# Replicated q and k copied in two halves by heads, maxima over six feed-forward blocks

## The chip, the core and the metric

One core of a Trainium2 chip runs the whole program. The metric is the device time in microseconds; lower is better. Engines are named TensorE (PE, with its weight loads PEld), VectorE (DVE), ScalarE (ACT), GpSimd (POOL) and SyncE (SP). Each has a queue of its own, executes it in order, and waits on semaphores.

## What is computed

Eight sequences x of 512 tokens with 256 channels each. First a cross attention with 16 heads on 64 context tokens, added to x. Then, of the normalised result, a dense path and a sparse path:

```python
q, k, v = x @ wq, x @ wk, x @ wv                     # 16 heads of 16
attn = softmax(where(causal, q k^T / 4, min))
h = x + rmsnorm((attn @ v) @ wo)
dense = h + rmsnorm((silu(h @ w1) * (h @ w3)) @ w2)   # 256 -> 1024 -> 256
probs = softmax(x @ router_w)                         # 8 experts, best 2 of each token
sparse = rmsnorm(sum(topw * expert(x)))
x = x + dense + sparse
```

## The kernel before

A sequence is a batch. The program walks the batches, and in walk b three things run interleaved: the cross attention of batch b, the causal attention's scores and the feed-forward network of batch b-1 (called c in the code), and then the projections q, k, v, the router and the maxima of batch b. Walk 0 has no batch before it and interleaves the keys and values of the context instead (steps `kv`). After the last walk the experts run over gathered tiles of tokens.

The order is one list of steps, `STEPS`, built by hand. Every engine walks the same list and takes from it the instructions that are its own, so the list is the order of each engine's queue, and semaphores (`need`, `done`, `before`) tie the engines together.

The causal attention wants the maximum of each row ahead of the exponentials. The scores are computed twice: once for the maxima only, in steps `max` (32 a batch: eight pairs of heads by four tiles of tokens; TensorE lines 969 and 970, reduced by VectorE in line 1540 from one of two pairs of PSUM banks, so that TensorE may be two maxima ahead), and again, a walk later, for the exponentials (`sc`). The maxima enter the second as rows of q: steps `shift_parts` and `shift` split and turn them (lines 1548 to 1555, TensorE line 979), SyncE sends them (`send_shifts`).

q and k are float32, and their products use bfloat16 in three parts. Steps `qk` 0 to 3 make q's two halves of heads, then k's (line 935); ScalarE, VectorE and GpSimd split each in three parts (lines 1196, 1199, 1481, 731). SyncE stores the twelve part tiles to DRAM (`parts_d`, line 537), and six copies each of q and k bring them back replicated (`q_rep`, `k_rep`, 96 rows): those of k by SyncE (line 544) after all its parts have landed, those of q by ScalarE in step `("route", 0)` (line 1220). Each copy has 16 rows of 16 KB, 256 KB. The two halves of the heads lie interleaved (`rep_at`). The first maximum waits for all twelve copies, and for the step `slots`.

Around it stand, in this order: `v` 0 to 3 (line 942; ScalarE copies the input for the second expert, line 1209, and the values, line 1213), between them `f_h_turn` (TensorE turns h of batch c, ScalarE copies it to `hT`, line 1146, VectorE makes its remainder, line 1570), `route` 0 to 2 (small operations of VectorE that choose two experts, lines 1490 to 1512), `fu` (up projections of block m of eight, line 1051, two each), `fg` (ScalarE's tanh, line 1253, VectorE's products, lines 1582 and 1591), `fd` (down projection, line 1061, two each), `slots` (TensorE lines 949 and 950, then VectorE's chain, lines 1521 to 1533, which gives each token its row) and `scatter` (GpSimd, line 747).

Of the kernel before, what the change touches and what calls it, by code (L numbers as in the profile page):

```python
# [10 lines left out]
ALU = mybir.AluOpType  # L11
# [4 lines left out]
BF16 = mybir.dt.bfloat16  # L16
# [27 lines left out]
K_PART = (0, 1, 0, 1, 2, 0)  # L44

UNITS = 10
CHUNKS = 3
# [8 lines left out]
    qk_ps=4, part1=4, rest1=4, part2=4, part3=4, v_ps=4, v_sb=4, lg=4,  # L56
    q_out=96, k_out=96, rep_q=96, rep_k=96, z=1,
    gmax=1, gexp=1, mask=1, rank_ps=1, slot=1, xk=1, scat=128, dve_step=42, pool_a=4, pool_n=1,
# [36 lines left out]
def interleaved():  # L95
# [18 lines left out]
]  # L114
_max = [("max", hp, t) for hp in range(H // 2) for t in range(T)]
for _m in range(3, FB):
    STEPS += [("fu", _m, 0)] + _max[:1] + [("fg", _m, 0), ("fu", _m, 1)] + _max[1:2]
    STEPS += [("fg", _m, 1), ("fd", _m - 1, 0)] + _max[2:4] + ([("shift", 0)] if _m == 6 else []) + [("fd", _m - 1, 1)] + _max[4:(5 if _m < 5 else 6)]
    STEPS += {5: [("shift_parts", 0)], 6: [("nx_stats",)], 7: [("nx_bq",), ("nx_apply",)]}.get(_m, [])
    _max = _max[(5 if _m < 5 else 6):]  # L120
STEPS += [_max[0], ("fd", FB - 1, 0), _max[1], ("fd", FB - 1, 1)] + _max[2:] + [
# [61 lines left out]
def score_bank(b):  # L183

    return 2 if b is None else 6


def rep_at(h):

    return h % (H // KD) * KD + h // (H // KD)  # L190

# [15 lines left out]
def xattn_ffn(nc, A, out):  # L207
    per = PER
    counted = {}
    with ExitStack() as ctx:  # L210
# [181 lines left out]
        vt_d = internal("vt_d", (PAIRS, P, B * CK))  # L392
        parts_d = internal("parts_d", (3, 2, HD, H // KD, KD, S), BF16)
        y_d = internal("y_d", (B, P, T, D))
# [41 lines left out]
        o_v = out.rearrange("b (t p) d -> b p t d", p=P)  # L436

        def at_batch(v, b):

            return v[b:b + 1, :, :, :].rearrange("a p t d -> p (a t) d") if isinstance(b, int) else v[bass.ds(b, 1), :, :, :].rearrange("a p t d -> p (a t) d")  # L440
# [7 lines left out]
        def _(sp):  # L448
            def load_x(b):
                before(sp, b, "xb")  # L450
                before(sp, b, "xn1")
                done(sp.dma_start(xin[:, :, :], at_batch(x_v, b)), "x_in", 16)

            def load_kv(b):
                before(sp, b, "vw_ps")
                for dst, src in ((k_bd, kt_d), (v_bd, vt_d)):
                    for i in range(2):
                        half = slice(i * CHD, (i + 1) * CHD)
                        done(sp.dma_start(dst[half, :, i * CK:(i + 1) * CK],
                                          src.rearrange("a p n -> p a n")[half, :, span(b, CK)]), "kv_in", 16)  # L460

            def send_shifts(b, i):
                first_head, end_head = SHIFTS[i]
                need(sp, b, "mT_sb", i + 1)
                for r in range(MROWS):
                    done(sp.dma_start(q_rep[KREP + r:KREP + r + 1, rep_at(first_head):rep_at(end_head - 1) + 1:KD, :],
                                      mT[r * H + first_head:r * H + end_head, i, :]), f"m_row{i}", 16)
# [55 lines left out]
            def batch(b, c, end=False, only=None):  # L523
# [5 lines left out]
                if b is not None:  # L529
                    if c is None:  # L530
                        load_late_weights()
                    elif b != B - 1:
                        load_kv(b + 1)
                    for a in range(4):
                        for i, name in enumerate(("part1", "part2", "part3")):
                            need(sp, b, name, a + 1)
                            done(sp.dma_start(parts_d[i, a // 2, :, :, a % 2, :].rearrange("d h n -> (d h) n"), parts[i][:, a, :]), ("q_out", "k_out")[a // 2], 16)
                    if c is not None:
                        need(sp, c, "b_ps", per["b_ps"])
                        sp.sem_inc(freed, 1)  # L540
                    need(sp, b, "k_out", per["k_out"])
                    for j in range(NREP):
                        src = parts_d[K_PART[j], 1, :, :, :, :].rearrange("d h a n -> d (h a n)")
                        done(sp.dma_start(k_rep[j:KREP:NREP, :, :].rearrange("d h n -> d (h n)"), src), "rep_k", 16)
                    if not (isinstance(b, int) and b == B - 1):
# [7 lines left out]
                    if c is None:  # L553
                        need(sp, b, "q_out", per["q_out"])
                        need(sp, b, "pv_ps", per["pv_ps"])
                        need(sp, b, "scat", per["scat"])
                        sp.sem_inc(freed, 1)
                        for dst, src in zip(w13_in, ("L0_ffn_w1", "L0_ffn_w3")):
                            sp.dma_start(dst, A[src].rearrange("(k p) n -> p k n", p=P)).then_inc(p0["w_up"], 16)
                    if b == B - 1:  # L560
                        need(sp, b, "pv_ps", per["pv_ps"])
                        need(sp, b, "q_out", per["q_out"])
# [241 lines left out]
        def _(pe):  # L804
# [31 lines left out]
            def batch(b, c, end=False, only=None):  # L836
# [10 lines left out]
                for step in only or walked(b, c, end):  # L847
# [77 lines left out]
                    elif kind == "qk":  # L925

                        a = step[1]
                        if a == 0:
# [3 lines left out]
                            need(pe, b, "xn2T", 2)  # L932
                        w = (wq, wk)[a // 2]
                        for k in range(KD):
                            last = mm(bank(a), w[:, k, a % 2 * P:(a % 2 + 1) * P], xn2T[:, k, :], start=(k == 0), stop=(k == KD - 1))
                        done(last, "qk_ps")
# [14 lines left out]
                    elif kind == "max":  # L951
# [3 lines left out]
                        if nmax == 0:  # L955
                            need(pe, b, "slot", 1)
                            need(pe, b, "rep_q", per["rep_q"])
                            need(pe, b, "rep_k", per["rep_k"])
                            if c is not None:
                                need(pe, c, "fu_g", 2)  # L960
                        elif nmax >= 2:
                            need(pe, b, "a_max", nmax - 1)
                        if nmax == 20:
                            need(pe, b, "mT_sb", 1)
                        n = (t + 1) * P
                        for i in range(2):
                            h = 2 * hp + i
                            o = nmax % 2 * 2 + i
                            mm(bank(o, n), q_rep[0:KREP, rep_at(h), t * P:n], k_rep[0:KREP, rep_at(h), 0:n], start=True, stop=False)  # L969
                            last = mm(bank(o, P, t * P), ident_b[:, :], mask_qk[:, :], start=False, stop=True)  # L970
# [10 lines left out]
                    elif kind == "sc":  # L981
# [11 lines left out]
                        for j, kb, at in score_rows(u):  # L993
                            o = (score_bank(b) + n % 2) * 512 + at
                            h = rep_at(4 * grp + j)
                            last = mm(ps[:, o:o + S - kb * P], k_rep[0:KREP + MROWS, h, kb * P:(kb + 1) * P], q_rep[0:KREP + MROWS, h, kb * P:S],  # L996
                               start=True, stop=True, skip_group_check=True)
# [133 lines left out]
        def _(act):  # L1131
# [9 lines left out]
            def batch(b, c, end=False, only=None):  # L1141
# [6 lines left out]
                for step in only or walked(b, c, end):  # L1148
# [44 lines left out]
                    elif kind == "qk":  # L1193
                        a = step[1]
                        need(act, b, "qk_ps", a + 1)
                        done(fn(parts[0][:, a, :], bank(a), ACT.Copy, scale=(HD ** -0.5 if a < 2 else 1.0)), "part1")
                        if a >= 1:
# [117 lines left out]
        def _(dve):  # L1315
# [72 lines left out]
            def batch(b, c, end=False, only=None):  # L1388
# [21 lines left out]
                for step in only or walked(b, c, end):  # L1410
# [56 lines left out]
                    elif kind == "qk":  # L1467
# [11 lines left out]
                        if a >= 2:  # L1479
                            need(dve, b, "part3", a - 1)  # L1480
                        done(v.scalar_tensor_tensor(rest[:, a % 2, :], bank(a), (HD ** -0.5 if a < 2 else 1.0), parts[0][:, a, :], ALU.mult, ALU.subtract), "rest1")
                    elif kind == "v":
# [198 lines left out]
```

How the kernel before makes its waits and increments, by code:

```python
        def need(eng, b, name, k):  # L403
            eng.wait_ge(sems[name], b * per[name] + k + AHEAD.get(name, 0))
# [1 line left out]
        def before(eng, b, name):  # L407
            if not (isinstance(b, int) and b == 0):
                eng.wait_ge(sems[name], b * per[name] + AHEAD.get(name, 0))
# [78 lines left out]
            def tiles(q, is_first, is_last):  # L489
                for i in range(LAST if is_last else 4):
                    row = sp.value_load(table[0:1, 1, span(q * 4 + i, 1)], min_val=0, max_val=E * REG)
                    if not is_first:
                        sp.wait_ge(moe["xT_ps"], q * 4 + i - 3)
                        sp.wait_ge(moe["ids"], q * 4 + i - 3)
                        sp.wait_ge(moe["gate"], q * 4 + i - 3)
                        sp.sem_inc(freed, 1)
                    sp.dma_start(xs[:, i, 0:D + 2], xs_d[bass.ds(row, P), 0:D + 2]).then_inc(xs_in[i], 16)
# [8 lines left out]
            def experts_first():  # L506
                sp.wait_ge(moe["table"], 2)
                for e in range(E):
                    row = sp.value_load(zero_row[0:1, e:e + 1], min_val=0, max_val=E * REG - P)
                    sp.dma_start(xs_d[bass.ds(row, P), 0:D], zeros[:, :]).then_inc(moe["zero"], 16)
# [2 lines left out]
                sp.dma_start(xs_d[E * REG:, D:D + 2], pad_rows[:, E, :].bitcast(F32), allow_slow_non_contiguous=True).then_inc(moe["zero"], 16)  # L514
                sp.wait_ge(sems["va_ps"], B * per["va_ps"])
                sp.wait_ge(sems["b_ps"], B * per["b_ps"])
                load_experts(range(EW_EARLY, E))
```

## Time and profile before

| | us |
|---|---|
| median of three runs | 1483.63 |
| runs | 1481.46 to 1485.07 |
| span of the profiled execution, first to last instruction | 1484.5 |
| TensorE busy in it | 1362.4 |
| VectorE, GpSimd, ScalarE busy | 810.0, 600.2, 575.1 |

For the profiled execution only its span is known, not the time of the run around it. One walk takes some 143 us, and seven of the eight look alike. A timeline row gives the start in microseconds, the duration of a merged group, engine and line, the tile written and the tiles read, the count, and in brackets how long the engine stood idle before it and who released it. The ends of matmuls are modelled. PEclk in a stretch is the granted clock of TensorE, 1.00 being full speed.

### The profile page before, as it was taken

The page shows a single profiled execution, that of the slowest core. Times are in us where ns is not written, and L with a number is a line of the kernel's source. Part 1 is how long each engine was busy: PE and PEld are TensorE (multiplying, and loading weights), DVE is VectorE, ACT ScalarE, POOL GpSimd, SP SyncE. Part 2 cuts the span into 40 slices and gives each one's busy share as a digit, 9 for nine tenths or more (in the row PEclk, how much of TensorE's full clock was granted, in tenths as well). Part 3 has the DMA queues.
Part 4 walks back from the last instruction along what each step waited for, and adds up shares of the span by engine and source line. Part 5 has one row for each costly group of instructions (what it writes and reads, how often), then busy time and mean ns, then how long its engine had stood idle before and what let it go on. Part 6 is the DMA issues. An engine that isn't in the chain of part 4 may idle for free. (4 is left out here: it accounts for less than half of the span.)

```text
span 1484.5 us, 22385 instructions
## 1 busy us (share of the span) xinstructions
PE 1362.4 (92%) x7229; PEld 882.2 (59%) x7230; DVE 810.0 (55%) x1654; ACT 575.1 (39%) x1214; POOL 600.2 (40%) x1051
## 2 busy tenths in 40 slices
PE   6887899899999989998999899999999889999995
PEld 5543556666665666566656665666566346666674
DVE  2625554764585368536753675467537623333348
ACT  2231553055306521642265126503640443344446
POOL 4312353254325342634254225423542445555544
PEclk9998899999999999999999999999999899999997
DMA  6053204110501050106000500140022533322245
GB/s 213 1 153 132 86 1 121 52 30 1 142 30 30 1 156 16 30 8 160 20 15 30 141 17 15 51 121 17 1 83 74 162 107 128 129 87 85 85 186 193
DMA packets 78297, 115.39 MB, mean 78 GB/s; under 512 B 24840, under 2 KB 66208, under 8 KB 75648
## 3 DMA queue, kind: packets, MB, share of 16 engines
q1 hardware_dynamic: 67888, 79.69, 17.9%
q10 hardware_dynamic: 3840, 16.78, 4.2%
q0 software_dynamic: 6480, 17.77, 3.3%
q8 instruction: 52, 0.85, 0.2%
q14 instruction: 37, 0.30, 0.1%
HBM read 70.22 MB, written 43.59 MB: 77 GB/s over the span
## 5 line engine op out<-in xcount | busy, mean ns | idle before, releaser
L1540 DVE TENSOR_REDUCE nm<-ps 128x2 f32<-128x256 f32 (+3 forms) x256 | 202.5, 819 | 85.6 <-PE ps L970 79.5
L1229 ACT ACTIVATE room<-ps 128x512 f32<-128x512 f32 x320 | 179.8, 599 | 151.3 <-PE ps L996 151.1
L1051 PE MATMUL ps<-hT,w 128*128 128x512 f32 x768 | 206.5, 412 | 0.0
L703 POOL TENSOR_SCALAR_AFFINE_SELECT room<-room 128x256 f32<-128x256 f32 (+1 forms) x320 | 121.0, 390 | 136.4 <-ACT room L1229 131.7
L969 PE MATMUL ps<-room 96*128 96x128 bf16 (+3 forms) x512 | 127.9, 312 | 35.7 <-DMA room<-parts_d 17.8
L1051 PEld LDWEIGHTS ps<-hT,w 128*128 128x128 f32 x768 | 140.4, 190 | 32.1 <-DVE hT L1570 2.0
L1061 PE MATMUL ps<-w,room 128*128 128x256 f32 x512 | 137.8, 400 | 7.8 <-DVE room L1591 7.8
L1253 ACT ACTIVATE room<-ps 128x512 f32<-128x512 f32 x64 | 37.2, 593 | 277.2 <-PE ps L1051 277.2
L1087 PE MATMUL ps<-room 128*128 x284 | 135.4, 599 | 1.8 <-ACT room L1281 1.8
L920 PE MATMUL ps<-room 128*128 128x256 f32 x512 | 123.1, 384 | 2.8 <-ACT room L1190 1.8
L901 PE MATMUL ps<-room,xnT 128*128 128x512 f32 x256 | 122.0, 601 | 0.0
L996 PE MATMUL ps<-room 99*128 99x384 bf16 (+3 forms) x512 | 111.0, 306 | 8.7 <-ACT room L1229 6.4
L969 PEld LDWEIGHTS ps<-room 96*128 96x128 bf16 x512 | 50.9, 100 | 97.9 <-DVE nm L1540 41.1
L920 PEld LDWEIGHTS ps<-room 128*128 128x128 f32 x512 | 93.8, 190 | 22.7 <-issue 6.7
L1061 PEld LDWEIGHTS ps<-w,room 128*128 128x128 f32 x512 | 91.9, 195 | 24.1 <-DVE room L1591 11.5
L970 PE MATMUL ps<-mask_qk,ident_b 128*128 128x128 bf16 x512 | 104.6, 225 | 0.0
L1634 DVE COPY room<-ps 128x256 f32<-128x256 f32 x71 | 30.1, 424 | 125.9 <-PE ps L1095 117.7
L1441 DVE TENSOR_TENSOR room<-ps,room 128x1024 f32<-128x1024 f32 x32 | 39.1, 1222 | 106.0 <-PE ps L901 106.0
L996 PEld LDWEIGHTS ps<-room 99*128 99x128 bf16 x512 | 42.9, 98 | 88.0 <-issue 44.7
L1009 PE MATMUL ps<-room,v_aug 128*32 128x512 f32 (+3 forms) x1024 | 90.6, 449 | 3.0 <-POOL room L703 2.0
L652 POOL TENSOR_TENSOR spare_p<-neg_half 128x1 f32<-128x1 f32 x95 | 18.3, 192 | 179.7 <-DVE room L1533 114.6
L794 POOL DMA_INDIRECT pair_d<-room,ids_u x71 | 71.8, 1011 | 33.7 <-issue 30.5
(236 smaller groups left out, 2360.1 us busy)
## 6 DMA issues: line engine op xcount, KB each, us to landing
room<-parts_d SPq DMA_DIRECT2D x48, 256.0 KB, 8.7
room<-parts_d ACTq DMA_DIRECT2D x48, 256.0 KB, 6.2
room<-xs_d SPq DMA_DIRECT2D x71, 129.0 KB
parts_d<-room SPq DMA_DIRECT2D x64, 128.0 KB, 1.8
room<-pair_d SPq DMA_DIRECT2D x8, 1024.0 KB, 7.8
room<-in_L_ffn_ew SPq DMA_DIRECT2D x24, 256.0 KB, 5.5
xin<-in_x SPq DMA_DIRECT2D x8, 512.0 KB, 11.3
parts_d<-xnT SPq DMA_DIRECT2D x32, 128.0 KB, 1.8
```

The source lines that it names most:

```text
L703: done(g.affine_select(out=w, in_=w, compare_op=ALU.is_ge, fill=0.0, base=0, pattern=[[0, 2]] * (blocks - 1) + [[1, P]], channel_multiplie ...
L901: last = mm(bank(half), xnT[:, k, t * P:(t + 1) * P], m_sb[:, k, half * 512:(half + 1) * 512], start=(k == 0), stop=(k == KD - 1))
L920: last = mm(bank(3, D), pT[:, t % 2, a * P:(a + 1) * P], vw[:, a, :], start=(a == 0), stop=(a == PAIRS - 1))
L969: mm(bank(o, n), q_rep[0:KREP, rep_at(h), t * P:n], k_rep[0:KREP, rep_at(h), 0:n], start=True, stop=False)
L970: last = mm(bank(o, P, t * P), ident_b[:, :], mask_qk[:, :], start=False, stop=True)
L996: last = mm(ps[:, o:o + S - kb * P], k_rep[0:KREP + MROWS, h, kb * P:(kb + 1) * P], q_rep[0:KREP + MROWS, h, kb * P:S], start=True, stop=T ...
L1009: last = mm(ps[32 * j:32 * j + 32, 4 * 512 + kb * P:5 * 512], v_aug[:, v_at(kb, 4 * grp + j):v_at(kb, 4 * grp + j) + 32], prob[:, at:at + ...
L1051: last = mm(bank(up_banks(b, m)[i]), w[:, x, k, m * P:(m + 1) * P], hT[:, y, k, :], start=((x, y, k) == terms[0]), stop=((x, y, k) == term ...
L1061: last = mm(bank((6, 7)[half], D, t % 2 * D), gT[:, m % 2, t * P:(t + 1) * P], w2[:, m, :], start=(m == 0 and t % 2 == 0), stop=(m == FB - ...
L1087: last = mm(bank(2 + i % 2), xsT[:, i % 2, k * P:(k + 1) * P], ew[:, bass.ds(at + k * 2 * D, 2 * D)], start=(k == 0), stop=(k == KD - 1))
L1229: done(fn(prob[:, u * 512:(u + 1) * 512], bank(score_bank(b) + n % 2), ACT.Exp), "b_exp")
L1540: done(v.tensor_reduce(nm[:, t, 2 * hp:2 * hp + 2], pair_ps, AX.X, ALU.max, negate=True), "a_max")
```

## The change

The heads are no longer interleaved: half 0 is heads 0 to 7, half 1 heads 8 to 15. The steps `qk` make q half 0, k half 0, q half 1, k half 1. SyncE stores the parts of half 0, waits until they have landed (`out_0`), copies k half 0, stores the parts of half 1, waits for `out_1`, and copies q and k of half 1. ScalarE copies q half 0, at the start of `("v", 0)` instead of in `("route", 0)`. There are 24 copies of 128 KB in the place of twelve of 256 KB. The first maximum waits for half 0 and maximum 16 for half 1. `slots` and `scatter` come directly behind `("fd", 0, 1)`, and the maxima are dealt over blocks 2 to 7 by the table `MAXIMA` instead of blocks 3 to 7; one maximum instead of two stands behind the last down step. The first turn of the shifts comes behind `("fu", 6, 0)` instead of in the middle of the down projection of that block.

```diff
+QK = ((0, 0), (1, 0), (0, 1), (1, 1))
...
-    q_out=96, k_out=96, rep_q=96, rep_k=96, z=1,
+    out_0=96, out_1=96, rep_0=192, rep_1=192, z=1,
...
-    ("fu", 2, 0), ("fg", 2, 0), ("fu", 2, 1), ("fg", 2, 1), ("slots",), ("scatter",), ("fd", 1, 0), ("fd", 1, 1),
+    ("slots",), ("scatter",),
 ]
+MAXIMA = {2: (1, 1, 1, 1), 3: (1, 1, 2, 1), 4: (1, 1, 2, 1), 5: (1, 1, 2, 2), 6: (1, 1, 2, 1), 7: (1, 1, 1, 1)}
 _max = [("max", hp, t) for hp in range(H // 2) for t in range(T)]
-for _m in range(3, FB):
-    STEPS += [("fu", _m, 0)] + _max[:1] + [("fg", _m, 0), ("fu", _m, 1)] + _max[1:2]
-    STEPS += [("fg", _m, 1), ("fd", _m - 1, 0)] + _max[2:4] + ([("shift", 0)] if _m == 6 else []) + [("fd", _m - 1, 1)] + _max[4:(5 if _m < 5 else 6)]
+for _m, _n in MAXIMA.items():
+    for _i, _s in enumerate((("fu", _m, 0), ("fu", _m, 1), ("fd", _m - 1, 0), ("fd", _m - 1, 1))):
+        STEPS += [_s] + ([("shift", 0)] if (_m, _i) == (6, 0) else []) + _max[:_n[_i]] + ([("fg", _m, _i)] if _i < 2 else [])
+        _max = _max[_n[_i]:]
     STEPS += {5: [("shift_parts", 0)], 6: [("nx_stats",)], 7: [("nx_bq",), ("nx_apply",)]}.get(_m, [])
...
-def rep_at(h):
-
-    return h % (H // KD) * KD + h // (H // KD)
...
-        parts_d = internal("parts_d", (3, 2, HD, H // KD, KD, S), BF16)
+        parts_d = internal("parts_d", (3, 2, KD, HD, H // KD, S), BF16)
...
+        def copy_part(eng, which, a):
+
+            rows = slice(a * (H // KD), (a + 1) * (H // KD))
+            for j in range(NREP):
+                src = parts_d[(Q_PART, K_PART)[which][j], which, a, :, :, :].rearrange("d h n -> d (h n)")
+                done(eng.dma_start((q_rep, k_rep)[which][j:KREP:NREP, rows, :].rearrange("d h n -> d (h n)"), src), ("rep_0", "rep_1")[a], 16)
...
+            def send_parts(b, half):
+                for n in (2 * half, 2 * half + 1):
+                    which, a = QK[n]
+                    for i, name in enumerate(("part1", "part2", "part3")):
+                        need(sp, b, name, n + 1)
+                        done(sp.dma_start(parts_d[i, which, a, :, :, :].rearrange("d h n -> (d h) n"), parts[i][:, n, :]), ("out_0", "out_1")[half], 16)
...
-                    for a in range(4):
-                        for i, name in enumerate(("part1", "part2", "part3")):
-                            need(sp, b, name, a + 1)
-                            done(sp.dma_start(parts_d[i, a // 2, :, :, a % 2, :].rearrange("d h n -> (d h) n"), parts[i][:, a, :]), ("q_out", "k_out")[a // 2], 16)
+                    send_parts(b, 0)
                     if c is not None:
                         need(sp, c, "b_ps", per["b_ps"])
                         sp.sem_inc(freed, 1)
-                    need(sp, b, "k_out", per["k_out"])
-                    for j in range(NREP):
-                        src = parts_d[K_PART[j], 1, :, :, :, :].rearrange("d h a n -> d (h a n)")
-                        done(sp.dma_start(k_rep[j:KREP:NREP, :, :].rearrange("d h n -> d (h n)"), src), "rep_k", 16)
+                    need(sp, b, "out_0", per["out_0"])
+                    copy_part(sp, 1, 0)
+                    send_parts(b, 1)
+                    need(sp, b, "out_1", per["out_1"])
+                    copy_part(sp, 0, 1)
+                    copy_part(sp, 1, 1)
...
-                            need(pe, b, "rep_q", per["rep_q"])
-                            need(pe, b, "rep_k", per["rep_k"])
+                            need(pe, b, "rep_0", per["rep_0"])
                             if c is not None:
                                 need(pe, c, "fu_g", 2)
                         elif nmax >= 2:
                             need(pe, b, "a_max", nmax - 1)
+                        if nmax == H // 4 * T:
+                            need(pe, b, "rep_1", per["rep_1"])
...
-                        done(fn(parts[0][:, a, :], bank(a), ACT.Copy, scale=(HD ** -0.5 if a < 2 else 1.0)), "part1")
+                        done(fn(parts[0][:, a, :], bank(a), ACT.Copy, scale=(1.0 if QK[a][0] else HD ** -0.5)), "part1")
...
+                            if c is not None:
+                                need(act, c, "b_ps", per["b_ps"])
+                            need(act, b, "out_0", per["out_0"])
+                            copy_part(act, 0, 0)
...
-                        if c is not None:
-                            need(act, c, "b_ps", per["b_ps"])
-                        need(act, b, "q_out", per["q_out"])
-                        for j in range(NREP):
-                            src = parts_d[Q_PART[j], 0, :, :, :, :].rearrange("d h a n -> d (h a n)")
-                            done(act.dma_start(q_rep[j:KREP:NREP, :, :].rearrange("d h n -> d (h n)"), src), "rep_q", 16)
```

## Rows read from the trace of the kernel before

**Rows 1.** The page: span, and busy time of each engine with its share.

```profile
span 1484.5 us, 22385 instructions
...
PE 1362.4 (92%) x7229; PEld 882.2 (59%) x7230; DVE 810.0 (55%) x1654; ACT 575.1 (39%) x1214; POOL 600.2 (40%) x1051
```

**Rows 2.** Waits of TensorE, 160 to 1160 us: who waited for whom, total us, times, longest.

```profile
PE ps L969 <- DMA room<-parts_d: 17.8, 7, 3.8
PE ps L969 <- DVE nm L1540: 8.0, 33, 0.5
...
PE ps L1061 <- DVE room L1591: 4.9, 7, 1.6
PE ps L979 <- DVE nm L1540: 4.1, 7, 0.6
PE ps L871 <- DVE nm L1540: 2.6, 6, 0.4
...
PE ps L969 <- DVE mT L1555: 1.1, 7, 0.2
```

**Rows 3.** Timeline, TensorE, batch 3: start, us, instructions, [idle before <- releaser].

```profile
531.03 5.87 PE L1051 MATMUL ps<-hT,w 128*128 128x512 f32 x24
537.43 1.99 PE L1061 MATMUL ps<-w,room 128*128 128x256 f32 x8 [0.53 <-DVE room L1591]
...
548.74 0.22 PE L969 MATMUL ps<-room 96*128 96x128 bf16 x1 [3.23 <-DMA room<-parts_d]
...
589.61 2.02 PE L871 MATMUL ps<-room 128*128 128x128 f32 x16 [0.44 <-DVE nm L1540]
```

**Rows 4.** Timeline, ScalarE and its queue, batch 3.

```profile
527.58 1.04 ACT L1209 ACTIVATE room<-xn_id 128x1024 f32<-128x1024 f32 x1
...
529.06 1.08 ACT L1146 ACTIVATE hT<-ps 128x512 fp32r<-128x512 f32 x2
...
531.46 3.71 ACTq L1220 DMA_DIRECT2D room<-parts_d  x6
```

**Rows 5.** Timeline, SyncE's queue, batch 3.

```profile
525.36 1.19 SPq L537 DMA_DIRECT2D parts_d<-room  x2
...
533.00 3.73 SPq L544 DMA_DIRECT2D room<-parts_d  x6
```

**Rows 6.** Timeline, VectorE, batch 3.

```profile
540.62 0.18 DVE L1504 TENSOR_REDUCE room<-small 128x4 f32<-128x32 f32 x1
...
542.56 0.69 DVE L1591 SCALAR_TENSOR_TENSOR room<-room,ps 128x512 f32<-128x512 f32 x1
543.16 0.74 DVE L1521 TENSOR_TENSOR ahead<-ahead,ps 128x8 f32<-128x8 f32 x4
...
545.90 0.17 DVE L1533 COPY room<-ids_all 128x4 uint32<-128x4 uint32 x1
```

**Rows 7.** Single lines: durations ns min/median/max, first and last start.

```profile
L586 SPq DMA_DIRECT2D room<-pair_d x8: 319/380/1387, 1433.0 to 1454.8; - x8
...
L1540 DVE TENSOR_REDUCE nm<-ps x256: 411/808/1225, 121.0 to 1162.9; 128x2 f32<-128x256 f32 x64, 128x2 f32<-128x768 f32 x64
```

**Rows 8.** Stretches: length, busy us by engine, PEclk, DMA share, GB/s.

```profile
538.00:542.00 4.00, 4.00 (x19) 3.18 (x17) 3.59 (x15) 0.60 (x1) 0.00 (x0) 1.00 1.09 262
...
834.00:838.00 4.00, 3.04 (x10) 2.17 (x10) 1.02 (x2) 0.00 (x0) 1.07 (x1) 0.50 0.15 45
```

**Rows 9.** Timeline, TensorE, batch 0.

```profile
105.12 7.13 PE L857 MATMUL ps<-room 128*128 128x512 f32 x16 [2.68 <-ACT hb L1156]
...
117.03 3.68 PE L857 MATMUL ps<-room 128*128 128x512 f32 x4 [4.74 <-ACT hb L1156]
```

**Rows 10.** Timeline, ScalarE, batch 0.

```profile
116.29 0.69 ACT L1156 ACTIVATE hb<-ps,bk 128x512 f32<-128x512 f32 x1 [6.75 <-DMA kt_d<-hb]
```

**Rows 11.** Timeline, TensorE, batch 5.

```profile
834.96 0.27 PE L969 MATMUL ps<-room 96*128 96x128 bf16 x1 [3.77 <-DMA room<-parts_d]
...
878.50 2.02 PE L871 MATMUL ps<-room 128*128 128x128 f32 x16 [0.43 <-DVE nm L1540]
```

More of the change, by code:

```diff
@@ L112 @@
     ("route", 1), ("fu", 1, 0), ("fg", 1, 0), ("fu", 1, 1), ("fg", 1, 1), ("route", 2), ("fd", 0, 0), ("fd", 0, 1),
[1 row of a table removed]
+    ("slots",), ("scatter",),
 ]
+MAXIMA = {2: (1, 1, 1, 1), 3: (1, 1, 2, 1), 4: (1, 1, 2, 1), 5: (1, 1, 2, 2), 6: (1, 1, 2, 1), 7: (1, 1, 1, 1)}
 _max = [("max", hp, t) for hp in range(H // 2) for t in range(T)]
-for _m in range(3, FB):
-    STEPS += [("fu", _m, 0)] + _max[:1] + [("fg", _m, 0), ("fu", _m, 1)] + _max[1:2]
-    STEPS += [("fg", _m, 1), ("fd", _m - 1, 0)] + _max[2:4] + ([("shift", 0)] if _m == 6 else []) + [("fd", _m - 1, 1)] + _max[4:(5 if _m < 5 else 6)]
+for _m, _n in MAXIMA.items():
+    for _i, _s in enumerate((("fu", _m, 0), ("fu", _m, 1), ("fd", _m - 1, 0), ("fd", _m - 1, 1))):
+        STEPS += [_s] + ([("shift", 0)] if (_m, _i) == (6, 0) else []) + _max[:_n[_i]] + ([("fg", _m, _i)] if _i < 2 else [])
+        _max = _max[_n[_i]:]
     STEPS += {5: [("shift_parts", 0)], 6: [("nx_stats",)], 7: [("nx_bq",), ("nx_apply",)]}.get(_m, [])
-    _max = _max[(5 if _m < 5 else 6):]
 STEPS += [_max[0], ("fd", FB - 1, 0), _max[1], ("fd", FB - 1, 1)] + _max[2:] + [
@@ L465, in send_shifts @@
                 for r in range(MROWS):
-                    done(sp.dma_start(q_rep[KREP + r:KREP + r + 1, rep_at(first_head):rep_at(end_head - 1) + 1:KD, :],
+                    done(sp.dma_start(q_rep[KREP + r:KREP + r + 1, first_head:end_head, :],
                                       mT[r * H + first_head:r * H + end_head, i, :]), f"m_row{i}", 16)
@@ L553, in batch @@
                     if c is None:
-                        need(sp, b, "q_out", per["q_out"])
                         need(sp, b, "pv_ps", per["pv_ps"])
@@ L561, in batch @@
                         need(sp, b, "pv_ps", per["pv_ps"])
-                        need(sp, b, "q_out", per["q_out"])
                         sp.sem_inc(freed, 1)
@@ L932, in batch @@
                             need(pe, b, "xn2T", 2)
-                        w = (wq, wk)[a // 2]
+                        which, half = QK[a]
+                        w = (wq, wk)[which]
                         for k in range(KD):
-                            last = mm(bank(a), w[:, k, a % 2 * P:(a % 2 + 1) * P], xn2T[:, k, :], start=(k == 0), stop=(k == KD - 1))
+                            last = mm(bank(a), w[:, k, half * P:(half + 1) * P], xn2T[:, k, :], start=(k == 0), stop=(k == KD - 1))
                         done(last, "qk_ps")
@@ L968, in batch @@
                             o = nmax % 2 * 2 + i
-                            mm(bank(o, n), q_rep[0:KREP, rep_at(h), t * P:n], k_rep[0:KREP, rep_at(h), 0:n], start=True, stop=False)
+                            mm(bank(o, n), q_rep[0:KREP, h, t * P:n], k_rep[0:KREP, h, 0:n], start=True, stop=False)
                             last = mm(bank(o, P, t * P), ident_b[:, :], mask_qk[:, :], start=False, stop=True)
@@ L994, in batch @@
                             o = (score_bank(b) + n % 2) * 512 + at
-                            h = rep_at(4 * grp + j)
+                            h = 4 * grp + j
                             last = mm(ps[:, o:o + S - kb * P], k_rep[0:KREP + MROWS, h, kb * P:(kb + 1) * P], q_rep[0:KREP + MROWS, h, kb * P:S],
@@ L1480, in batch @@
                             need(dve, b, "part3", a - 1)
-                        done(v.scalar_tensor_tensor(rest[:, a % 2, :], bank(a), (HD ** -0.5 if a < 2 else 1.0), parts[0][:, a, :], ALU.mult, ALU.subtract), "rest1")
+                        done(v.scalar_tensor_tensor(rest[:, a % 2, :], bank(a), (1.0 if QK[a][0] else HD ** -0.5), parts[0][:, a, :], ALU.mult, ALU.subtract), "rest1")
                     elif kind == "v":
```

## Prediction

> **What bounds the kernel now.** I read the busy table first: TensorE is busy for 92% of a span of 1484.5 us [rows 1], so only its idle time and the order that causes it can move. Then the waits of TensorE over the seven batches that run beside the feed-forward of the batch before (160 to 1160 us) [rows 2]. Four things stand out there: 17.8 us for the replicated q and k to land (2.54 us a batch), 4.9 us in the down projection (0.70), and, while the maxima run, 8.0 us for the reduce of VectorE, 4.1 us before the turn of the shifts, 1.1 us behind its copy and 2.6 us at the region's end: 15.8 us, 2.26 a batch. Together 5.50 us a batch, 38.5 us in seven. That is all this change can win there; the region's arithmetic stays. Last I read one batch as a timeline of each engine [rows 3 to 6], because the change reorders, and what counts is who is late after it.
>
> In that batch (number 3) TensorE goes straight from the fourth value step into the up projections at 531.03, waits 0.53 at 537.43, and stands 3.23 us before the first maximum at 548.74; the next batch begins at 589.61 [rows 3]. The way the copies reach their queues is the second thing to see: ScalarE issues six of 256 KB from 531.46 on and is held 3.71 us by it [rows 4], SyncE issues the six of k at 533.00 [rows 5].
>
> **Part 1, the copies of q by ScalarE move from the first route step to the first value step.** Six part stores (q and k of half 0) have been issued by 526.55: the last of the pair in [rows 5] starts near 526.2. The last part store of the batch starts near 531.25 and its landing releases SyncE at 533.00 [rows 5], so a landing takes 1.75 us and half 0 is out at about 528.0. ScalarE is there at 527.6, so it waits 0.4 us, then issues six copies, and only then does it make the copy for the second expert, the first two value copies, and the two copies of hT [rows 4]. The first up projection waits for hT. In the trace hT is just in time (copies done at 530.1, VectorE's remainder after it, TensorE free at 531.03 [rows 3, 4]), so each us that ScalarE is late is a us of TensorE. Behind the wait stand on ScalarE: the expert copy, v_sb and hT; behind these VectorE's hT remainder, its logits and the router.
>
> How long six issues take is the term that the trace does not show: the new copies are 8 KB a row, not 16 KB. Upper end: 0.62 each, as now [rows 4], 3.7 us, delay 4.2. Lower end: 0.38, that of the loads from pair_d, which also have 8 KB contiguous on both sides [rows 7], 2.3 us, delay 2.75. No gain is possible here, as the six are still issued ahead of hT. I take 0.455 with its gap, nearer to the pair_d row because the row length is the same: 2.7 us, delay 3.2. So TensorE waits 3.2 us (2.75 to 4.2) where it waited for nothing.
>
> What the move removes: the six issues stood between the up projection and its tanh, and the route. With them gone the 0.70 us wait of the down projection goes.
>
> **Part 2, slots before the third block.** Take the delay of 3.2. Up projections start at 534.25; the first two steps end at 537.2 (5.87 us for four [rows 3]), the second product of VectorE at 538.1 (0.69 each [rows 6]), route step 1 is nine small operations of 0.22 (540.0), the two products of block 1 follow (541.35), then route step 2, six operations of 0.22 from the row at 540.62 on [rows 6], so the mask is ready at 542.65. TensorE has done blocks 0 and 1 at 540.2 and the down projection (1.65) at 541.95: it waits 0.75 for the mask. Before, block 2 stood in between. VectorE's slot chain runs from 543.16 to 546.07, 2.91 us [rows 6]; after 0.3 us for the product to arrive it now ends at 545.9. TensorE covers 1.5 of it with one step of block 2, ends at 544.2 and waits 1.7. Bounds: if the product of block 1 is seen 0.5 earlier both waits lose that once; if GpSimd holds VectorE up, as long as that, they grow as much. The scatter by GpSimd follows the slots, and its first entries are released by the maxima as before; nobody waits for it in either order.
>
> **Part 3, the copies by halves.** Half 0 leaves at 528.0 on both queues, 12 copies of 128 KB. The engines moved 262 GB/s while the old copies and the load of x ran [rows 8]; 1.57 MB take 6 to 6.5 us, so half 0 is there at 535 to 537, nine us before the first maximum can run. The 2.54 us wait goes. SyncE issues its six copies of k ahead of the six part stores of half 1, which land near 538; then twelve copies, some 6 us of issue, then x of the next batch and the shifts. Half 1 lands near 547, x near 551; maximum 16 comes after 560, x is read after 575. This edit has one answer: hidden, by more than ten us.
>
> **Part 4, maxima over six blocks.** I replayed the orders of TensorE and VectorE through the region, TensorE never more than two maxima ahead, with reduces of 0.42 to 1.22 by their width, 0.81 in the middle [rows 7]. For the old order this gives 4.3 us of waits where the trace names 2.26. For the new order it gives 3.7: the four double maxima become fewer and the wait at the end shrinks, but the turn of the shifts now stands behind one up step only (1.1, for the parts of the shifts) and maximum 20 directly behind it (0.85, for the copy). Scaled by 2.26/4.3 that is 1.95. Ends: 1.07 (only the turn and its copy) and 3.0.
>
> **Part 5, batch 0.** It has no feed-forward; TensorE waits 2.68 and 4.74 us for ScalarE, and its eleventh key/value step takes 3.68 us after the second, where the four before took 7.13 [rows 9]. The reason of the second wait is in [rows 10]: the store to kt_d lands 6.75 us late, behind 1.57 MB of q on ScalarE's own queue, issued just before it. In the new order that queue holds half as much and ten us earlier. Walking it: ScalarE comes to the first key/value copy 3.2 us later, TensorE loses 1.3 at the third of these steps, then runs four steps in 7.1 as in [rows 9] without the two waits; slots at 110.6 for 112.1, first maximum at 114.0, when the slot chain ends, for 120.55. Gain 6.5, and 5.5 if issues cost 0.62; I take 6.0. It stays, since the weights that hold the end of this batch are loaded behind it in the same order.
>
> **The sum.** A batch: 3.2 + 0.75 + 1.7 + 1.95 = 7.60 added, 5.50 removed, 2.1 slower; seven of them 14.7. Batch 0 saves 6.0, and behind the last batch one reduce less is outstanding, 0.4. Net 8.3 us. The span, 1484.5, lies inside the runs (1481.46 to 1485.07), and 0.9 above their median; what lies around it is not shown. So 1483.6 + 8.3 = 1491.9 us.
>
> **The clock.** After the wait of 3.77 us before 834.96 the granted clock was 0.50 for four us [rows 8, 11], the lower of the levels, 1.2 GHz, and that region took 43.5 us (to 878.50 [rows 11]) for the 40.9 of batch 3: 2.7 us. After the 3.23 us in batch 3 it stayed at 1.00. So a wait of this length may or may not cost 2.7 us more. I leave the number of such falls as it is; none at all would save some 4 (that region, and one more that lost less), one in every batch would add 14.
>
> **Rivals.** (a) The issues are free: ScalarE's six issues do not delay hT, or the part stores land early. Then a batch adds 4.4 and loses 5.5, seven save 7.7, with batch 0 and the end 14.1: 1469.5. The point where it turns is a stall at hT of 2.0 us for no change (7 x (2.0 - 1.1) = 6.4) and of 1.35 for 0.3% faster. For it speaks that SyncE's queue is quick; against it that [rows 4] shows 3.71 us for six, and that hT has no slack.
> The Trainium skill (DMA: Bandwidth & Descriptors, Issuing engines are not separate DMA queues) says that the sequencer's time to start a DMA is usually small beside the DMA; by that rule the stall is small and (a) holds. The trace does not agree: the issuing engine is held as long as in [rows 4].
> (b) Cheap issues and short waits: 2.75 + 0.75 + 1.7 + 1.07 = 6.27, 0.8 a batch, 5.4 less 6.9: 1482.1, and 1478 if no clock fall is left.
> (c) Every hT stall makes the clock fall: 1491.9 + 14 = 1506. For it: the stall is longer than most of today's; against: 3.23 passed unharmed.
> (d) The order doesn't do what it says, half 0 or half 1 not there in time: it would need a landing nine (or thirteen) us later than by [rows 8]; then the old wait of 17.8 us stays, 1509.
>
> **How the numbers follow.** Forecast with its own range 1487 to 1499 (issue 0.38 to 0.62): 0.52. (a) 0.11. (b) 0.21. (c), with falls in some batches, 0.13. (d) 0.03. The range 1476 to 1503 leaves out most of (a), the far part of (c) and (d). About 0.3% (4.5 us) is what a measurement can tell here: faster (below 1479.2) is (a) and a little of (b), 0.14; same takes most of (b) and the low edge of the forecast, 0.26; slower 0.60.
>
> **What would show it.** Right: a wait near 3 us of TensorE before the first up projection, for hT; ScalarE's issues directly after its last part copy; no wait for parts_d; waits for the mask and for the slot row before block 2; first maximum of batch 0 near 114. Wrong: hT's copies start before 531 in the window of batch 3, six issues in under 1.5 us, or the waits in the region of maxima rise above 3 us.

## The result and the profile after

The changed kernel takes 1515.2 us (median of four, 1513.75 to 1519.24) against 1483.93 of the kernel before: a ratio of 1.021, 95% interval 1.019 to 1.023. It is 31.3 us slower; in the profiled executions 27.5 (1512.0 for 1484.5). The forecast was 8 us slower.

The page of the changed kernel: the span, the busy time of the engines, and the group of the up projections (busy, mean ns, idle before them and its releaser).

```profile
span 1512.0 us, 22481 instructions
...
PE 1363.9 (90%) x7229; PEld 888.0 (59%) x7230; DVE 801.6 (53%) x1654; ACT 576.0 (38%) x1214; POOL 600.5 (40%) x1051
...
L1062 PE MATMUL ps<-hT,w 128*128 128x512 f32 x768 | 216.7, 427 | 31.4 <-DVE hT L1579 31.4
```

TensorE's work is the same, and its busy time nearly so [rows 1]: 1.5 us more, while its idle time grew by 26.0, from 122.1 to 148.1. That idle time has a new first entry, ahead of the up projections. The waits of TensorE in the seven batches beside a feed-forward (160 to 1180 us), as in [rows 2]:

```profile
PE ps L1062 <- DVE hT L1579: 31.4, 7, 5.0
PE ps L980 <- DVE room L1542: 10.6, 7, 1.5
PE ps L990 <- DVE nparts L1560: 6.5, 7, 0.9
PE ps L959 <- DVE maskb L1521: 5.7, 7, 0.9
...
PE ps L980 <- DVE mT L1564: 4.2, 7, 0.6
PE ps L853 <- DVE room L1441: 4.2, 6, 0.7
PE ps L980 <- DVE nm L1549: 3.3, 20, 0.2
```

The wait for the copies, 17.8 us before, is gone, and so is that of the down projection. New are hT (31.4 us, 4.5 a batch), the slot row (10.6), the mask (5.7), the parts of the shifts (6.5) and a wait of the next batch's second turn (4.2). One batch on TensorE, the same as in [rows 3]:

```profile
541.28 8.49 PE L1062 MATMUL ps<-hT,w 128*128 128x512 f32 x24 [4.39 <-DVE hT L1579]
549.61 1.89 PE L1072 MATMUL ps<-w,room 128*128 128x256 f32 x8
552.16 0.19 PE L959 MATMUL ps<-maskb,before_b 128*128 128x32 bf16 x1 [0.67 <-DVE maskb L1521]
...
555.39 0.23 PE L980 MATMUL ps<-room 96*128 96x128 bf16 x1 [1.52 <-DVE room L1542]
...
584.13 0.40 PE L990 MATMUL ps<-ident_b,nparts 128*128 128x128 bf16 x4 [0.94 <-DVE nparts L1560]
585.13 0.22 PE L980 MATMUL ps<-room 96*128 96x128 bf16 x1 [0.60 <-DVE mT L1564]
...
600.11 2.02 PE L880 MATMUL ps<-room 128*128 128x128 f32 x16
...
605.13 0.63 PE L853 MATMUL ps<-ident,room 128*128 128x128 f32 x4 [0.70 <-DVE room L1441]
```

VectorE ahead of that last wait, the scaling of the feed-forward's result and then the copy that TensorE waits for:

```profile
602.73 1.66 DVE L1633 SCALAR_TENSOR_TENSOR room<-ps,ri,fw_bc 128x256 f32<-128x256 f32 x4 [0.31 <-POOL ri L672]
604.30 1.28 DVE L1441 COPY room<-ps 128x512 f32<-128x512 f32 x2
```

The up projections of blocks 0 and 1 wait 4.39 us and then take 8.33 us to the next row, where they took 6.4 with the down projection's wait included. ScalarE in the same batch, against [rows 4]:

```profile
532.78 0.63 ACT L1213 ACTIVATE room<-xin 128x512 bf16<-128x512 f32 x1 [0.35 <-DVE xin L1490]
533.74 3.96 ACTq L441 DMA_DIRECT2D room<-parts_d  x6
537.82 1.06 ACT L1224 ACTIVATE room<-xn_id 128x1024 f32<-128x1024 f32 x1 [4.41 <-issue]
...
539.31 1.08 ACT L1157 ACTIVATE hT<-ps 128x512 fp32r<-128x512 f32 x2
```

Its last part copy starts at 532.78, the six issues run from 533.74 to 537.8, and hT is copied from 539.31 on, while TensorE stands. SyncE's queue, against [rows 5]: half 0 of k from 533.68, and the twelve copies of half 1.

```profile
533.68 3.71 SPq L441 DMA_DIRECT2D room<-parts_d  x6
...
544.75 7.46 SPq L441 DMA_DIRECT2D room<-parts_d  x12
```

And the granted clock in three stretches of 4 us there, the stall in the first (length, busy of TensorE first, PEclk is the third number from the end):

```profile
538.00:542.00 4.00, 0.72 (x2) 0.62 (x3) 1.81 (x6) 3.06 (x8) 0.92 (x1) 0.79 1.03 246
542.00:546.00 4.00, 4.00 (x11) 3.13 (x10) 0.69 (x1) 0.70 (x2) 0.00 (x0) 0.50 0.47 161
546.00:550.00 4.00, 4.00 (x16) 3.19 (x16) 2.83 (x11) 0.60 (x1) 0.00 (x0) 0.86 0.74 225
```

The clock falls to 0.50, the level of 1.2 GHz, for the four us behind the stall (0.86 in the next four); after the 3.23 us of [rows 3] it had stayed at 1.00. Batch 0 on TensorE, against [rows 9]:

```profile
96.81 1.98 PE L866 MATMUL ps<-room 128*128 128x512 f32 x4 [2.14 <-ACT hb L1167]
...
99.52 12.18 PE L866 MATMUL ps<-room 128*128 128x512 f32 x28
...
114.75 0.23 PE L980 MATMUL ps<-room 96*128 96x128 bf16 x1 [1.20 <-DVE room L1542]
```

The third key/value step waits 2.14 us, the next seven run without a pause, and the first maximum starts at 114.75, where it started near 120.55.

### The profile page after: what moved, and what is told of

Its sections match the earlier page's. It is cut to its first block and busy times, and to the rows that moved or that the text cites. A ratio compares the mean times of both kernels' runs of the same rounds, so it can differ in the third digit from the quotient of the medians.

```text
span 1512.0 us, 22481 instructions
## 1 busy us (share of the span) xinstructions
PE 1363.9 (90%) x7229; PEld 888.0 (59%) x7230; DVE 801.6 (53%) x1654; ACT 576.0 (38%) x1214; POOL 600.5 (40%) x1051
## 5 line engine op out<-in xcount | busy, mean ns | idle before, releaser
L1062 PE MATMUL ps<-hT,w 128*128 128x512 f32 x768 | 216.7, 427 | 31.4 <-DVE hT L1579 31.4
L1062 PEld LDWEIGHTS ps<-hT,w 128*128 128x128 f32 x768 | 146.7, 201 | 66.1 <-DVE hT L1579 34.3
L980 PE MATMUL ps<-room 96*128 96x128 bf16 (+3 forms) x512 | 128.2, 310 | 27.1 <-DVE room L1542 11.8
L1072 PE MATMUL ps<-w,room 128*128 128x256 f32 x512 | 134.3, 390 | 2.9 <-DVE room L1600 2.9
```

The costliest lines, as they stand in the source:

```text
L980: mm(bank(o, n), q_rep[0:KREP, h, t * P:n], k_rep[0:KREP, h, 0:n], start=True, stop=False)
L1062: last = mm(bank(up_banks(b, m)[i]), w[:, x, k, m * P:(m + 1) * P], hT[:, y, k, :], start=((x, y, k) == terms[0]), stop=((x, y, k) == term ...
L1072: last = mm(bank((6, 7)[half], D, t % 2 * D), gT[:, m % 2, t * P:(t + 1) * P], w2[:, m, :], start=(m == 0 and t % 2 == 0), stop=(m == FB - ...
```

## The experiments

All times are medians. The kernel before was run again beside the experiments and took 1480 to 1485 us; the ratios, with their 95% intervals, are against it. Where two experiments, or one and the changed kernel, are compared, they may have run on different chips, and the number in brackets is the difference by the ratios. Three theories: (1) ScalarE's issues ahead of hT hold TensorE, and its clock falls behind the stall; (2) the new place of slots and maxima is the loss; (3) many small copies are the loss.

### One part undone: the issues back in the route step

```diff
 elif kind == "v":                                  # ScalarE, t == 0
-    need(act, b, "out_0", per["out_0"]); copy_part(act, 0, 0)
 elif kind == "route" and step[1] == 0:
+    need(act, b, "out_0", per["out_0"]); copy_part(act, 0, 0)
     need(act, b, "gmax", 1)
```

> The changed kernel with one part undone: ScalarE issues its six copies of q half 0 in the first route step, behind hT, as before. Theory 1 (the issues ahead of hT hold TensorE and let its clock fall): the 4.5 us wait for hT goes in seven batches, the clock falls go with it (about 1.5 us each), but the tanh stands behind the issues again and the mask comes later against TensorE: waits of about 0.7, 2.8 and 1.7 us. About 1494 us. Theory 2 (the new order of slots and maxima is the loss): hardly faster than the changed kernel, 1510 us. Theory 3 (24 small copies in the place of 12 are the loss): 1510 us or more.

1502.0 us, ratio 1.012 (1.008 to 1.017). Its waits of TensorE, 160 to 1165 us:

```profile
PE ps L959 <- DVE maskb L1521: 17.9, 7, 2.6
PE ps L980 <- DVE room L1542: 8.3, 7, 1.5
...
PE ps L1072 <- DVE room L1600: 4.8, 7, 1.4
```

The wait for hT is gone and a part of the loss with it, but the mask now costs 2.56 a batch: with hT in time, TensorE reaches the slots step sooner, while the issues delay the tanh and all that follows on VectorE. The six issues hold ScalarE as before, only at another place. It came out between theories 1 and 2, 8 us above theory 1. The three waits are not the reason, they are 0.69, 2.56 and 1.19 us a batch for some 0.7, 2.8 and 1.7 expected. The clock is: I had expected its falls to go, and it fell behind the wait for the mask in five of the seven batches. In the first of them:

```profile
252.00:256.00 4.00, 2.37 (x8) 1.56 (x8) 3.18 (x17) 0.00 (x0) 0.00 (x0) 0.76 0.68 209
256.00:260.00 4.00, 3.39 (x12) 2.24 (x12) 1.71 (x6) 0.60 (x1) 1.28 (x2) 0.50 0.75 185
```

TensorE was busy for 1366.9 us in it, and for 1347.6 in the next experiment.

### The copies of q half 0 on SyncE's queue

```diff
+copy_part(sp, 0, 0)
 copy_part(sp, 1, 0)                                # SyncE
-copy_part(act, 0, 0)                               # ScalarE, ("v", 0)
```

> The changed kernel with ScalarE's six copies of q half 0 issued by SyncE instead, ahead of those of k half 0; ScalarE issues no copies in the batches. Theory 1: no wait for hT, no clock fall; the waits for mask (0.8) and slots (1.5) and those among the maxima (2.0) stay, 4.9 us a batch against 5.5 of before, and batch 0 keeps its 6 us: 1470 to 1476 us. Theory 2: waits for mask and slots grow, 1500 us or more. Theory 3: the copies arrive late as one queue issues all, a wait for the copies of about 3 us returns: 1490 us.

1470.7 us, ratio 0.994 (0.991 to 0.997): 44 us (40 by the ratios) faster than the changed kernel by one move. No wait for hT is left; the up projections' busy time is 204.2 us for 216.7, and that of TensorE as a whole 1347.6 for 1363.9. The kernel before had 1362.4, so it too lost much to the clock: of the 18.5 us by which this span (1466.0) is shorter than its, 14.8 are busy time. The longest waits in the seven batches:

```profile
PE ps L981 <- DVE room L1539: 10.6, 7, 1.5
PE ps L960 <- DVE maskb L1518: 10.4, 7, 1.5
PE ps L991 <- DVE nparts L1557: 6.5, 7, 0.9
```

Slots and parts are as in the changed kernel, the mask 1.5 a batch for 0.8. Theory 1 holds; theory 3 falls, as all 24 copies are still there and none is waited for.

### The early issue alone, in the kernel before

```diff
 elif kind == "v":                                  # ScalarE, t == 0
+    need(act, b, "q_out", per["q_out"])
+    for j in range(NREP): ... act.dma_start(q_rep[j:KREP:NREP, :, :] ...)
 elif kind == "route" and step[1] == 0:
-    need(act, b, "q_out", per["q_out"])
-    for j in range(NREP): ... act.dma_start(q_rep[j:KREP:NREP, :, :] ...)
```

> The kernel before with one part of the change alone: ScalarE issues its six 256 KB copies of q in the first value step instead of the first route step. Theory 1: a wait of 4.5 us for hT in seven batches, with clock falls of 1.5, against 2.5 (copies) and 0.7 (tanh) that go, and some 4 us gained in batch 0: about 1500 us. Theory 2 and theory 3: no slower than before, 1478 to 1484 us.

1501.8 us, ratio 1.012 (1.007 to 1.017), with whole copies, the old order of heads and the old steps. The wait in seven batches:

```profile
PE ps L1051 <- DVE hT L1570: 30.1, 7, 5.0
```

This one change of place makes the stall by itself. No wait for the copies is left in this trace, whole as they are.

### The copies alone, with the old steps

```diff
-("slots",), ("scatter",),                          # behind ("fd", 0, 1)
+("fu", 2, 0), ("fg", 2, 0), ("fu", 2, 1), ("fg", 2, 1), ("slots",), ("scatter",), ("fd", 1, 0), ("fd", 1, 1),
-MAXIMA over blocks 2 to 7
+maxima over blocks 3 to 7, as before
```

> The changed kernel's copies in two halves, ScalarE's at the first value step, with the step list of the kernel before (slots behind block 2, maxima over five blocks). Theory 1: the wait for hT and the clock falls stay, 4.5 and 1.5 us, the waits for mask (0.8) and slots (1.5) and the one at the next batch's first turns (0.6) go: about 1497 us, so the copies are two thirds of the loss. Theory 2: about 1484 us. Theory 3: as the changed kernel, 1515 us.

1500.2 us, ratio 1.013 (1.009 to 1.017). So the new steps cost 15 us (12) of the changed kernel on top of the copies. Waits, 160 to 1180 us:

```profile
PE ps L1061 <- DVE hT L1578: 31.6, 7, 5.2
PE ps L979 <- DVE nm L1548: 8.1, 34, 0.5
```

Mask, parts and the next batch's turn are not among them; the maxima wait for their reduces 8.1 us here and 3.3 in the changed kernel. That is what dealing them over six blocks won, and the turn of the shifts, the wait behind its copy and the one at the region's end gave 3.4 of it back: 7.3 us together here, 10.7 there.

### The stall filled with work

```diff
 if m == 0:                                         # TensorE, ("fu", 0, 0)
+    if i == 0 and b is not None:
+        for _ in range(10):
+            mm(bank(4), wq[:, 0, 0:P], xn2T[:, 0, :], start=True, stop=True)
     need(pe, c, "hT_lo", 2)
```

> The changed kernel with ten products of 128x512 added on TensorE ahead of its wait for hT, in the batches that run beside a feed-forward; their result is overwritten. They fill the 4.4 us stall and change no order. Theory 1a (the stall itself costs 4.5 us a batch, and the clock that falls after it 1.5 to 2.5 us more): the wait shrinks to under 0.5 us, the up projections come back from 7.4 to 8.5 us to 5.9 us, and 10 to 15 us of the changed kernel's 1515 go: 1500 to 1505 us. Theory 1b (the up projections are slow for another reason, such as the copies running beside them): the granted clock or the times stay as they are, 1515 us.

1531.0 us, ratio 1.035 (1.030 to 1.039), 16 us (20) slower than the changed kernel. TensorE in the batch shown above:

```profile
542.93 8.75 PE L1052 MATMUL ps<-xn2T,wq 128*128 128x512 f32 x20
551.12 6.16 PE L1065 MATMUL ps<-hT,w 128*128 128x512 f32 x24
```

My ten products took 8.2 us, not 4.3: they were twice as long as the stall, so the time by itself is no test. The second row is one: behind them the up projections take 6.16 us, with the copies in flight as before. The time fits it: seven times 3.8 us more than the stall are 27 us, 16 (20) were measured, so some 11 (7) came back. The run was repeated with five.

> The changed kernel with five products of 128x512 added on TensorE ahead of its wait for hT. The ten added before ran 8.3 us, twice the stall; five run about 4.2 us and just fill it. Theory 1a: the wait is under 0.6 us, the up projections take 5.9 to 6.2 us for the 7.6 of the changed kernel, and seven times 1.7 us, 12 us, go: 1503 us. Theory 1b: 1515 us.

1504.5 us, ratio 1.013 (1.011 to 1.014), with `range(5)`:

```profile
532.44 4.46 PE L1052 MATMUL ps<-xn2T,wq 128*128 128x512 f32 x10
537.00 5.87 PE L1065 MATMUL ps<-hT,w 128*128 128x512 f32 x24
```

The stretch from 168 to 1190 us (length, busy of TensorE first, PEclk third from the end):

```profile
168.00:1190.00 1022.00, 968.31 (x5485) 631.83 (x5484) 583.69 (x1194) 386.53 (x769) 387.32 (x565) 1.00 0.19 55
```

In six of the seven batches the work ends just when hT is there, in one 1.36 us are still waited. The up projections take 5.87 us in the place of 7.1 to 8.5, and the granted clock is 1.00 over the 1022 us. Nothing else differs from the changed kernel, so 10.7 us of it (13) are the clock, 1.5 a batch. This is what the falls cost altogether, not what they cost more than in the kernel before, which had falls of its own.

### Half of ScalarE's issues

```diff
-copy_part(act, 0, 0)                               # ScalarE: six
+copy_part(act, 0, 0, range(3))                     # ScalarE: three
+copy_part(sp, 0, 0, range(3, NREP))                # SyncE: three, ahead of k
```

> The changed kernel with three of ScalarE's six copies of q half 0 issued by SyncE. If the stall is the issue time, it shrinks by three times 0.61 us, from 4.5 to 2.6 us: 13 us less, 1502 us, and if the clock falls in fewer of the batches after a stall of that length, down to 1490 us. If the stall is the wait for the landed parts and not the issues, it stays above 4 us: 1513 us.

1489.0 us, ratio 1.004 (1.002 to 1.006). Two of its seven waits for hT, with the up projections behind them:

```profile
241.14 5.87 PE L1063 MATMUL ps<-hT,w 128*128 128x512 f32 x24 [2.46 <-DVE hT L1580]
...
529.26 7.41 PE L1063 MATMUL ps<-hT,w 128*128 128x512 f32 x24 [2.47 <-DVE hT L1580]
```

The wait is 2.46 us in all seven batches, 17.3 in sum: it follows the issues. Five of the seven kept 5.87 us behind it, two fell to 7.4; in the changed kernel, behind 4.4 to 5.0 us, all seven were slow. So the clock's price grew with the stall's length, and three issues less bring 26 us (26) where the stall alone gives 14. The profiles differ by 24.7: 14.1 are the stall, 7.0 TensorE's busy time (1356.9 for 1363.9), and 2 of the rest are idle time of batch 0, where ScalarE issues three copies less as well.

### Whole copies, all on SyncE

```diff
+need(sp, b, "q_out", per["q_out"])                 # SyncE, between the part stores of q and of k
+for j in range(NREP): ... sp.dma_start(q_rep[j:KREP:NREP, :, :] ...)
-for j in range(NREP): ... act.dma_start(...)       # ScalarE, ("route", 0)
```

> The kernel before with one thing changed: the six 256 KB copies of q are issued by SyncE once the parts of q have landed, ahead of the part stores of k, and ScalarE issues none. It keeps whole copies and the old steps. The wait of the down projection (0.7) goes; the copies of k start near 538 and land near 546.5, so 1 to 2 us of the wait for the copies stay; batch 0 gains about 6: 1466 us. If the halves are what hides the copies, this is slower than the 1453 of halves with the old steps by 7 times 1.5 us. If the issuing engine alone decides, it is equal to it, 1453 us.

1494.8 us, ratio 1.007 (1.005 to 1.008). I expected 1466. SyncE's queue in one batch:

```profile
525.57 3.71 SPq L542 DMA_DIRECT2D room<-parts_d  x6
529.33 0.58 SPq L545 DMA_DIRECT2D parts_d<-xnT  x1
...
536.83 3.65 SPq L549 DMA_DIRECT2D room<-parts_d  x6
```

The part stores of k stand behind 1.57 MB of q on the same queue and land 5 us after they are issued. The copies of k start 13 us after the last part of q was issued (near 523.8), where it was 7 in [rows 5], and every first maximum waits for it, 4.1 us a batch:

```profile
PE ps L974 <- DMA room<-parts_d: 29.0, 7, 5.3
```

TensorE's busy time, 1365.4 us, shows that its clock fell too. Moving the issues off ScalarE is thus not enough in this order of the queue, where k's parts stand behind q's copies; all twelve whole copies behind all part stores were not tried.

### Halves on SyncE, with the old steps and with mended ones

The first has the diff of the second experiment and that of the fourth together.

> All copies on SyncE in two halves, with the step list of the kernel before. Of 5.5 us a batch that waited before, the copies' 2.5 and the down projection's 0.7 go, some 0.4 comes back for slots: 2.8 a batch, 20 us, and 6 to 7 in batch 0, and the two clock falls: 1453 us. If the new steps are worth anything with the copies out of the way, this is slower than the 1470.7 of the kernel with all copies on SyncE and the new steps; by the waits it is faster by 15 us.

1453.1 us, ratio 0.981 (0.977 to 0.985), as expected. It is 17.6 us (20) faster than the same copies with the new steps, and 41.8 (38) faster than whole copies on SyncE with the old steps, 12.5 of it TensorE's busy time (1352.9 for 1365.4). This pair differs in the order of the heads and of the part stores too, not only in the size of the copies. The Trainium skill (Perfetto Trace Analysis, DMA Optimizations) says that splitting DMAs into smaller chunks may let some start sooner, and the whole be done sooner where the DMA engines are generally idle; this pair, 1453.1 against 1494.8 us, agrees with it.

```diff
-("slots",), ("scatter",),                          # behind ("fd", 0, 1)
+("fu", 2, 0), ("slots",), ("scatter",), ("fg", 2, 0), ("fu", 2, 1), ("fg", 2, 1),
+("fd", 1, 0), ("fd", 1, 1), ("max", 0, 0), ("max", 0, 1),
+MAXIMA = {3: (1, 1, 2, 1), 4: (1, 1, 2, 1), 5: (1, 1, 2, 2), 6: (1, 1, 2, 2), 7: (1, 1, 1, 1)}
-("shift", 0) behind ("fu", 6, 0)
+("shift", 0) behind ("fu", 6, 1) and its maximum
```

> All copies on SyncE, and the step list mended: slots behind the first up step of block 2, two maxima behind its last down step, then (1,1,2,1), (1,1,2,1), (1,1,2,2), (1,1,2,2), (1,1,1,1) in blocks 3 to 7, four behind, and the turn of the shifts behind the second up step of block 6. If the waits that the trace of the kernel with all copies on SyncE names are independent, mask (1.5), slots (1.5), parts (0.9) and most of the copy of the shifts (0.5) and the next batch's turn (0.3) go, and 0.5 to 1 us come back among the maxima: 3.5 to 4 us a batch, 1445 us. If VectorE as a whole is what bounds the region, they come back as waits for its reduces: 1465 us or more.

1445.0 us (median of six), ratio 0.975 (0.972 to 0.978): 2.5% faster than the kernel before and 4.5% than the changed one. The waits that are left around the maxima in the seven batches:

```profile
PE ps L981 <- DVE nm L1546: 5.8, 21, 0.5
...
PE ps L981 <- DVE mT L1561: 4.1, 7, 0.6
PE ps L881 <- DVE nm L1546: 2.6, 6, 0.4
```

No mask, no slots, no parts. VectorE does not bound the region: its reduces cost TensorE 1.2 us a batch with the one at the end.

## Why the prediction was wrong, step by step

The sign was right and so was the kind of the largest cost; the sizes were not: 8.3 us forecast, 31.3 measured, 12 us above the range's end. In the profiles it is 27.5, so 19.2 are to be accounted for. Two steps failed, the price of ScalarE's issues and the clock, and a wait was missing from the sum. Below are the six walks of batches 1 to 6, each counted from its first product of q, in the kernel before, the changed kernel and the second experiment (length, busy of TensorE, and PEclk third from the end):

```profile
233.20:1093.80 860.60, 813.98 (x4670) 538.96 (x4669) 505.75 (x1020) 330.85 (x660) 336.25 (x486) 0.99 0.19 52
229.40:1116.40 887.00, 817.80 (x4669) 543.96 (x4669) 498.54 (x1020) 331.61 (x660) 335.86 (x486) 0.98 0.17 50
223.90:1076.30 852.40, 806.01 (x4669) 535.84 (x4668) 507.97 (x1020) 331.42 (x660) 336.59 (x486) 1.00 0.17 52
```

These walks grew by 4.4 us each for 2.1 forecast, 3.8 of it idle time and 0.6 busy time: 13.8 of the 19.2. The walk of batch 0 saved 3.8 for 6.0 (2.2), and the walk of batch 7 with all behind it grew by 4.9 for 1.7 (3.2).

- **ScalarE's copies (part 1).** The largest failed term. Right in kind, and the wait for the landing was 0.45 us (0.4 forecast). The issues were mis-sized: I took 0.455 each with its gap, near the 0.38 of the loads of pair_d, because these too have 8 KB rows. The new copies took 0.61 in the instruction and 0.66 with the gap, and the old ones of 16 KB rows 0.61 as well: between 8 and 16 KB the row length does not set this price. My upper end, 4.2, was still below the 4.5 measured. This term missed 1.3 a batch, 9 us.
- **The clock.** The second failed step, and smaller than it looks. I left the number of falls as it was, at one and a weaker one. In the kernel before the granted clock was below 1.00 behind three of the seven waits for the copies (3.00, 3.77 and 2.34 us; not behind 3.23, 2.17, 1.73 and 1.59), in the changed kernel behind all seven stalls. In the second experiment it was at 1.00 in all six walks of the table. Against its 806.0 us of busy time the kernel before has 8.0 us more and the changed one 11.8, which I put down to the falls: 3.8 more. The last stretch gives 2.0 back, and over the whole execution TensorE's busy time rose by 1.5. So my "one in every batch would add 14" was wrong as well: it rests on 2.7 us a fall, where they came to 2.0 on average, and on some 4 us of them in the kernel before, where there were twice as many. The ends of the stall and the clock also belong together, and I widened the range for one at a time: my 4.2 with a fall in each batch gives 1513.
- **A wait at the next batch's second turn.** Not in the sum: 4.2 us. It waits for VectorE's copy in line 1441, which stands behind the scaling of line 1633. With one maximum instead of two behind the last down step, less work lies over the chain from that step by way of GpSimd to the scaling. I had counted only the reduce that goes. The experiments that keep two maxima there show the wait at most once; the one maximum was not changed alone.
- **Mask and slots (part 2).** 0.81 and 1.51 a batch, 0.75 and 1.7 forecast: right.
- **Copies by halves (part 3).** Right: no wait for a copy in any batch.
- **Maxima (part 4).** 6.5, 4.2 and 3.3 us are 2.0 a batch for 1.95. The sum is right, its split is not: the turn and the wait behind its copy were to be 1.03 (1.95 of the 3.7, scaled) and were 1.53, the reduces 0.92 and were 0.47. That both errors cancel is luck.
- **Batch 0 (part 5).** The first maximum came 5.8 us earlier for 6.0, at 114.75. That it stays was wrong: when the next walk begins its projections, 3.8 are left.

9.0 + 4.2 + 2.2 for batch 0 + 1.5 of busy time, less 1.3 for the slots, are 15.6 of the 19.2. The other 3.6 lie in smaller waits and in the last stretch and were not traced to a term. In the runs the difference is 3.8 us more than in the profiles. A run's time is 1.8 us above its span (1513.75 and 1512.0), so the profiled execution of the kernel before counts as a run of 1486.3, 2.4 above its median, while that of the changed kernel was its fastest run, 1.45 below its median.

Of the rivals, (a), that the issues are free, fell: the third experiment costs 22 us (17) for their place alone. The rule of the Trainium skill named beside it (DMA: Bandwidth & Descriptors, Issuing engines are not separate DMA queues) does not carry to an engine whose next instruction is the one that all wait for: an issue of 0.61 us is indeed small beside the 4.6 us to its landing, but six of them stand in the chain. The second experiment, where the issues are off ScalarE, came out at 1470.7 us, near the 1469.5 of (a), but by other terms: the mask cost 1.5 a batch for 0.75, and TensorE's busy time was 14.8 us below that of the kernel before, which (a) left as it was. Of (c) the condition came true, a fall behind every stall, and its price did not.

## What to carry to other kernels

A DMA that is issued from a computing engine costs that engine the issue time of every copy, and the price is charged to whoever waits for its next instruction: count it in that chain, at the price of the nearest copy of the same kind, or give it to a queue that computes nothing. A stall and the fall of the clock behind it are one term, and here they grew together, faster than the stall. What the clock costs already has to be read from whole walks against a trace without falls, not from one stretch: the kernel before lost twice what I had read. A step put ahead in the order needs the same look as a transfer: what covered its input before, and what covers it now.

## What the runs showed of the hardware beside that

- The issue of a replicated copy with 16 rows takes a median of 0.611 us on ScalarE at 256 KB and at 128 KB alike, and 0.59 on SyncE. Why loads with 128 rows take 0.38 was not tried.
- Part stores queued behind 1.57 MB of copies on SyncE's own queue landed after a median of 5.1 us in the batch shown, and after 1.8 in the kernel before.
- The length of a wait alone did not decide whether the clock fell. Behind waits of 2.46 us the up projections were slow twice in seven times, behind 2.56 us the granted clock fell five times in seven, in the kernel before it fell behind 2.34 us and not behind 3.23. Behind 4.4 us and more the up projections were slow seven times in seven, and never with the wait filled by products whose result nobody reads.
